# Attention B in another slot order, with the first sequences' rows gathered in the stage before and the last scatters a sequence earlier

## What is computed

```python
x = x + attn_a(layernorm(x))          # 16 heads, 12 of them over a window
x = x + ffn(layernorm(x))             # "first FFN"
x = x + attn_b(layernorm(x))          # "attention B"
x = x + ffn(layernorm(x))             # "second FFN", the same weights

# ffn: 16 experts, four are taken for every row, and a shared one for all rows
hid = relu2(einsum('th,eih->eti', flat, W1)); y = einsum('eti,ehi->eth', hid, W2)
out = einsum('eth,te->th', y, cw) + relu2(flat @ Ws1.T) @ Ws2.T

# attn_b: D = 512, chunks of 128 rows, four of them in a sequence of 512 rows
q, k, v = x @ Wq + bq, x @ Wk + bk, x @ Wv + bv; gate = sigmoid(x @ Wg + bg)
local = softmax(causal(q @ k.T * scale)) @ v       # inside a chunk
cross = q @ (sum of k.T @ v over the earlier chunks)
out = ((local + cross) * gate) @ Wo + bo
```

## Time and profile before

| what | value |
|---|---|
| median of 3 runs | 3603.19 us (3586.75 to 3605.06) |
| profiled execution | 3567.86 us |
| its span | 3566.1 us |
| mean granted TensorE clock | 0.913 |

### The profile page before, as it was taken

The page is one execution under the profiler, slowest core; times in us unless marked ns, Lnnn a source line. Parts: engine busy times, 40 slices in busy tenths (PEclk is TensorE's granted clock), DMA queues, the critical chain, the costliest instruction groups (busy, mean ns, idle before and its releaser), DMA issues. The chain is left out here.

```text
span 3566.1 us, 59187 instructions
## 1 busy us (share of the span) xinstructions
PE 2901.0 (81%) x17728; PEld 2204.3 (62%) x17728; DVE 2236.6 (63%) x5557; ACT 1598.9 (45%) x3092; POOL 1407.1 (39%) x1606
## 2 busy tenths in 40 slices
PE   6989889889977678988749888888888828899982
PEld 4655565555555467878736666666666618778871
DVE  8878777778747567754435656557557344456653
ACT  3554544545542145656524343333433316556650
POOL 2323233233240644443154223555453235545545
PEclk9999999999987689999969999999998959999996
DMA  1211212112013356767632112332332246778873
GB/s 63 79 44 57 71 50 75 48 49 79 37 52 121 130 189 214 241 228 257 215 92 65 54 60 65 101 99 91 99 99 68 68 169 237 256 249 282 287 243 119
DMA packets 206294, 454.65 MB, mean 127 GB/s; under 512 B 28304, under 2 KB 119568, under 8 KB 204944
## 3 DMA queue, kind: packets, MB, share of 16 engines
q1 hardware_dynamic: 156816, 316.37, 26.0%
q0 software_dynamic: 49152, 134.28, 11.5%
HBM read 215.15 MB, written 234.88 MB: 126 GB/s over the span
## 5 line engine op out<-in xcount | busy, mean ns | idle before, releaser
L370 POOL TENSOR_SCALAR_AFFINE_SELECT a_pt<-a_pt 128x512 f32<-128x512 f32 (+1 forms) x320 | 178.3, 557 | 687.9 <-ACT a_pt L470 687.2
L1723 POOL DMA_INDIRECT b_yg<-made,k_picks x256 | 250.7, 979 | 412.6 <-DVE b_xin L1874 342.3
L1024 POOL DMA_INDIRECT slots<-f_xn,k_picks x256 | 254.7, 995 | 329.4 <-PE f_XT L1463 124.8
L470 ACT ACTIVATE a_pt<-a_S 128x384 f32<-128x384 f32 (+3 forms) x640 | 254.7, 452 | 258.7 <-PE a_S L767 255.1
L2461 POOL DMA_INDIRECT f_yg<-made,k_picks x256 | 255.9, 1000 | 233.3 <-PE f_XT L2642 120.3
L617 DVE TENSOR_REDUCE a_mx<-a_FB 128x2 f32<-128x384 f32 (+4 forms) x512 | 276.1, 591 | 51.1 <-PE a_FB L745 37.4
L2187 PE MATMUL b_FB<-b_xh,b_wl 128*128 128x512 f32 x384 | 167.6, 437 | 129.7 <-DVE b_xl L2110 110.4
L1733 POOL DMA_INDIRECT slots<-b_staged,k_picks x192 | 192.5, 1003 | 186.6 <-PE b_FB L2189 71.5
L739 PE MATMUL a_FB<-a_kb,a_qb 128*128 128x192 bf16 (+4 forms) x1024 | 204.2, 264 | 59.7 <-DVE a_mx L617 52.0
L767 PE MATMUL a_S<-a_qs,a_ks 97*128 97x384 f32 (+3 forms) x640 | 180.6, 360 | 35.7 <-ACT a_pt L470 20.4
L780 PE MATMUL a_PV<-a_pt,a_vv 128*32 128x192 f32 (+4 forms) x2048 | 197.1, 367 | 2.7 <-POOL a_pt L377 2.6
(11 more groups left out here) (395 smaller groups left out, 7701.8 us busy)
## 6 DMA issues: line engine op xcount, KB each, us to landing
f_xg<-slots SPq DMA_DIRECT2D x160, 512.0 KB
made<-f_ye SPq DMA_DIRECT2D x160, 512.0 KB
slots<-a_zeros SPq DMA_DIRECT2D x16, 2560.0 KB, 9.2
a_xin<-in_x SPq DMA_DIRECT2D x16, 512.0 KB, 10.1
x_after_a<-a_xres SPq DMA_DIRECT2D x16, 512.0 KB, 2.9
f_xin<-x_after_a SPq DMA_DIRECT2D x16, 512.0 KB
f_wexp<-in_w_exp SPq DMA_DIRECT2D x8, 1024.0 KB, 12.8
bases<-f_xin SPq DMA_DIRECT2D x16, 512.0 KB
```

The lines of the kernel that those rows point to most:

```text
L470: nc.scalar.activation(pt[:, u % 4, b * w:(b + 1) * w], S[:, s_bank[2 * u + b], 0:w], ACT.Exp).then_inc(e_done, 1)
L1024: nc.gpsimd.indirect_dma_start(out=slots[s // BATCH][:, :], out_offset=bass.IndirectOffsetOnAxis(ap=picks[:, i:i + 1], axis=0), in_=xn[:, ...
L1723: nc.gpsimd.indirect_dma_start(out=yg[:, b, k, :], out_offset=None, in_=made[s // BATCH][:, :], in_offset=bass.IndirectOffsetOnAxis(ap=rou ...
```

## The change

The rows of sequences 0 and 1 are gathered on GpSimd in steps 61 to 64 and 68 to 71 of the first FFN; their bases are loaded by SyncE at step 59 into `xin`, and VectorE combines sequence 0 behind steps 63 to 66. `yg` and `xin` are therefore shared by both stages. Attention B starts without them; sequence 1 is combined there in the body of -1. In attention B the front's two T move from slots 2 and 3 to 0 and 1, K and V products alternate, the routing's transposes and logits stand two and one slots later, ranks and choice one. The scatters of sequences 0 to 8 stay where they were; 9 and 10 both go into the body of 14, out of `yg`, which no gather uses any more, and 11 into the body of 15. The last body, 16, has none.

```diff
@@ -846,6 +846,7 @@
...
+        self.yg, self.xin = sb("yg", [P, TB, TOP_K, H]), sb("xin", [P, 2, TB, H])
...
@@ -1009,10 +1013,15 @@
...
+                    if v == G_AT - 2:
+                        for s in range(2):
+                            sp.wait_ge(b_stored[s], 16)
+                            sp.dma_start(xnext[:, s], rows(base_d, s)).then_inc(next_loaded, 16)
...
@@ -1048,6 +1057,18 @@
...
+                def gather(s, b):
+                    if s == 0 and b == 0:
+                        for i in range(2):
+                            pool.wait_ge(ye_stored[i], 16 * NSTEP // 2)
+                    if s:
+                        pool.wait_ge(c_step, TOP_K * (b + 1))
+                    for k in range(TOP_K):
+                        i = s * PICKS + b * TOP_K + k
+                        nc.gpsimd.indirect_dma_start(
+                            out=yg[:, b, k, :], out_offset=None, in_=made[0][:, :],
+                            in_offset=bass.IndirectOffsetOnAxis(ap=picks[:, i:i + 1], axis=0)).then_inc(gathered[b], 16)
...
+                    for s, first in ((0, G_AT), (1, G_AT + TB + 3)):
+                        if first <= T - E_AT < first + TB:
+                            in_step(T)
+                            gather(s, T - E_AT - first)
+                for b in range(TB):
+                    pool.wait_ge(gathered[b], 2 * 16 * TOP_K)
...
@@ -1366,6 +1393,17 @@
...
+                def combine(b):
+                    dve.wait_ge(gathered[b], 16 * TOP_K)
+                    if b == 0:
+                        dve.wait_ge(next_loaded, 32)
+                    for k in range(TOP_K):
+                        j = b * TOP_K + k
+                        if k:
+                            dve.wait_ge(c_step, j)
+                        nc.vector.scalar_tensor_tensor(out=xnext[:, 0, b, :], in0=yg[:, b, k, :], scalar=wall[:, j:j + 1],
+                                                       in1=xnext[:, 0, b, :], op0=ALU.mult, op1=ALU.add).then_inc(c_step, 1)
...
@@ -1401,6 +1439,8 @@
...
+                    if G_AT + 2 <= v < G_AT + 2 + TB:
+                        combine(v - G_AT - 2)
...
@@ -1526,15 +1566,16 @@
...
-    FRONT = [("T", 0), ("T", 1)] + [(c, i) for c in "qkvg" for i in range(DT)]
+    FRONT = ([("T", 0), ("T", 1)] + [("q", i) for i in range(DT)] + [(c, i) for i in range(DT) for c in "kv"] +
+             [("g", i) for i in range(DT)])
...
-    FRONT_SLOT = (2, 3, 4, 5, 6, 7, 8, 9, 10, 11, 12, 13, 14, 15, 16, 17, 18, 19)
...
-    ROUTE_AT = {4: ("rT0", "rT1"), 7: ("rL",), 15: ("rX",)}
+    ROUTE_AT = {6: ("rT0", "rT1"), 8: ("rL",), 16: ("rX",)}
...
@@ -1559,8 +1600,11 @@
...
-    MOMENT_SLOT, RLOG_SLOT, SCALE_SLOT, GROUP_SLOT, CHOOSE_SLOT, PLACE_SLOT, TABLE_SLOT = 15, 1, 2, 10, 11, 16, 17
-    RES_SLOT, SCATTER_SLOT = 8, (9, 12, 15, 18)
+    MOMENT_SLOT, RLOG_SLOT, SCALE_SLOT, GROUP_SLOT, CHOOSE_SLOT, PLACE_SLOT, TABLE_SLOT = 15, 1, 2, 10, 12, 17, 18
+    RES_SLOT, SCATTER_SLOT, SCATTER_SLOTS = 8, (9, 12, 15, 18), (4, 6, 8, 10, 12, 14, 16, 18)
+    LAST = nseq - BATCH - 1
+    SCATTERS = {s: (s - BATCH - 1,) for s in range(BATCH + 1, nseq - 2)}
+    SCATTERS.update({nseq - 2: (LAST - 2, LAST - 1), nseq - 1: (LAST,)})
...
@@ -1682,15 +1727,18 @@
...
-                    if 0 <= s - BATCH - 1 < nseq - BATCH:
-                        at_least(sp, scattered, 16 * PICKS * (s - BATCH - 1))
-                        sp.dma_start(staged[:], seq_rows(sp, xn_d, s - BATCH - 1)).then_inc(st_loaded, 16)
+                    for i in SCATTERS.get(s, ()):
+                        if i in (LAST - 2, LAST - 1):
+                            sp.wait_ge(c_step, PICKS * (nseq - 1))
+                            sp.dma_start(yg[:, LAST - 1 - i], seq_rows(sp, xn_d, i)).then_inc(yg_loaded[LAST - 1 - i], 16)
+                        else:
+                            at_least(sp, scattered, 16 * PICKS * i)
+                            sp.dma_start(staged[:], seq_rows(sp, xn_d, i)).then_inc(st_loaded, 16)
...
-                sp.dma_start(xin[:, 0], seq_rows(sp, base_d, 0)).then_inc(x_loaded, 16)
...
@@ -1707,8 +1755,6 @@
...
-                sp.wait_ge(x_loaded, 16)
-                sp.dma_start(xin[:, 1], seq_rows(sp, base_d, 1)).then_inc(x_loaded, 16)
...
@@ -1716,8 +1762,7 @@
...
-                    if s:
-                        pool.wait_ge(c_step, PICKS * (s - 1) + TOP_K * (b + 1))
+                    pool.wait_ge(c_step, PICKS * (s - 2) + TOP_K * (b + 1))
...
@@ -1727,36 +1772,39 @@
...
-                        pool.wait_ge(st_loaded, 16 * (s + 1))
+                        if s in (LAST - 2, LAST - 1):
+                            pool.wait_ge(yg_loaded[LAST - 1 - s], 16)
+                        else:
+                            pool.wait_ge(st_loaded, 16 * (s + 1 if s < LAST else LAST - 1))
+                    src = yg[:, LAST - 1 - s] if s in (LAST - 2, LAST - 1) else staged
...
-                            in_=staged[:, b, :], in_offset=None).then_inc(scattered, 16)
+                            in_=src[:, b, :], in_offset=None).then_inc(scattered, 16)
...
                 def body(s, par, core, front, ahead):
                     for e in range(NSLOT):
...
-                            pool.wait_ge(c_step, PICKS * (s + 2))
+                            at_least(pool, c_step, PICKS * (s + 1))
...
-                        if e in SCATTER_SLOT and 0 <= s - BATCH - 1 < nseq - BATCH:
+                        mine = SCATTERS.get(s, ())
+                        at = SCATTER_SLOT if len(mine) == 1 else SCATTER_SLOTS
+                        if mine and e in at:
                             if front:
                                 pool.wait_ge(f_done, filled(s + 1, FRONT_AT[e][0]))
-                            scatter(s - BATCH - 1, SCATTER_SLOT.index(e))
+                            scatter(mine[at.index(e) // TB], at.index(e) % TB)
...
-                for s in range(2):
-                    for b in range(TB):
-                        gather(s, b)
...
@@ -1864,13 +1912,13 @@
...
-                    dve.wait_ge(gathered[b], 16 * TOP_K * (s + 1))
+                    at_least(dve, gathered[b], 16 * TOP_K * (s - 1))
                     if b == 0:
-                        dve.wait_ge(x_loaded, 16 * (s + 1))
+                        at_least(dve, x_loaded, 16 * (s - 1))
                     for k in range(TOP_K):
                         j = s * PICKS + b * TOP_K + k
                         if k:
-                            dve.wait_ge(c_step, j)
+                            dve.wait_ge(c_step, j - PICKS)
...
@@ -2149,7 +2197,7 @@
...
-                        if ahead and e in C_SLOT:
+                        if ahead and s + 2 >= 1 and e in C_SLOT:
                             combine(s + 2, C_SLOT.index(e))
```

More of the change, by code:

```diff
@@ L932, in phase_f @@
         ye_stored = [sem("ye_stored%d" % i) for i in range(2)]
+        gathered, next_loaded, c_step = [sem("gathered%d" % i) for i in range(TB)], sem("next_loaded"), sem("c_step")
         NCONST = 12
+        G_AT = NV - NSTEP + 1
         def used(sem, ring, i):
@@ L1651, in phase_b @@
         n_stored, st_loaded, scattered = sem("n_stored"), sem("st_loaded"), sem("scattered")
+        yg_loaded = [sem("yg_loaded%d" % i) for i in range(2)]
         NSTAT = TB + 10
```

11 lines of the change are left out of this document (7 added, 4 removed).

## The result

| what | before | changed |
|---|---|---|
| median (4 runs each, same chip) | 3594.97 us (3582.12 to 3605.06) | 3534.66 us (3526.17 to 3540.37) |
| ratio, 95% interval | | 0.9833, 0.9803 to 0.9863 |
| profiled span, mean granted clock | 3566.1 us, 0.913 | 3538.6 us, 0.919 |

The change is 60 us faster; forecast were 116. The time lies inside the outer range of 3430 to 3555, but outside the 3455 to 3520 that the forecast gave itself. The two profiled executions lie only 27 us apart, because the one of before was a fast one of its kernel (27 us under its median).

The account below looks back on a forecast made before the run. TensorE, busy 81% of the span, was taken to bound the kernel, with time to gain at the handover, in attention B and at its end. Terms -43.5 + 8 - 75 - 5 = -115.5 gave 3487 us, own range 3455 to 3520.

Parts of the forecast that it names:

- Term 1: Handover into attention B: first product 13.8 us behind the first transfer instead of 59.0; minus 43.5 us taken, bounds 35 and 48.
- Term 2: First FFN's last twenty steps: 32 gathers and the combines put in there cost plus 8 us, bounds 0 and 15.
- Term 3: Attention B's sequences: earlier T casts and alternating K and V save 5 us a sequence, fifteen times, 75 us.
- "Fifteen times": Attention B: the 5 us gain of one sequence was counted for all fifteen, giving 75 us.
- The clock: One attention B sequence: a shorter wait before slow-clock products gains 0.7 to 1.3 us, booked as 1.
- "K and V alternate": Attention B: small waits at V and gate products shrink by 1 us; a K copy behind table loads costs 0.7.
- Term 4: End of attention B: scatters moved up a sequence shorten the 10 us with nothing busy; minus 5, bounds 0 and 10.
- A: Rival: attention B's VectorE chain is longer through the shared port lock, 2.4 us in each of fifteen sequences; 3523 us, chance 0.14.
- "it just misses": Attention B: GpSimd's addition ends at 38.4 us of the sequence, VectorE's scaling comes at 38.5, so they do not meet.
- C: Rival: attention B's granted clock stays low for 15 us after each of two waits a sequence; slower, 3703 us, chance 0.04.
- D: Rival: attention B's second T cast still waits for softmax and tables, gain waited at V; 1 us a sequence, 3547, chance 0.08.
- B: Rival: attention B's waits fall below what slows the clock and bank waits go; 3 us more per sequence, 3442, chance 0.12.

Follow-up runs that it names:

- the last experiment: Changed kernel with last scatter group in slot 19, K products ahead of V, and two sequences' scatters moved from body 14 to 15: 3463.93 us, 0.9739 of the kernel before.
- the best kernel: Changed kernel with the last scatter group in slot 19 instead of 18 and K products ahead of V again: 3453.81 us, 0.9719 of the kernel before.
- the order alone: Kernel before with only attention B's new slot order; gathers, combine, handover and scatters as before: 3524.60 us, 0.9895 of the kernel before.

## Why the prediction was right in direction and twice too large

**Term 1, handover (-43.5): right, measured -39.0.** The first product stands 15.5 us behind the first transfer, 13.8 were forecast, released by the second weight piece's low half, as said; the wait for piece 3 is 1.45 us (1.7). D(0) comes 28.3 us behind the first product instead of 23.8, with a wait of 1.1 at a copy of V and a clock of 0.90.

```profile
1805.88 2.35 POOL L1810 TENSOR_TENSOR b_wl<-b_raw,b_wh 128x1024 fp32r<-128x1024 f32 x1 [3.67 <-ACT b_wh L1858]
1808.33 0.77 PE L2235 MATMUL b_FB<-b_xh,b_wl 128*128 128x512 f32 x1 [3.24 <-POOL b_wl L1810]
...
1819.46 0.47 PE L2235 MATMUL b_FB<-b_wh,b_xl 128*128 128x512 f32 x1 [1.45 <-POOL b_wl L1810]
```

**Term 2, the first FFN (+8): right in kind, about 12.** Four executions without the gathers took 155 to 166 us from the thirtieth-last load, ten with them 167 to 181: means 161.2 and 172.9. At the first gathers a tile load comes late; whether the gathers or the two row loads issued just ahead of them (1688.5), which the prediction had at nothing, hold it up, no run separates. Behind that each of the four steps with a combine takes 4.7 to 5.0 us instead of 4.4, since the tile's copy on VectorE stands behind it. Both in the changed kernel:

```profile
1698.12 1.09 PE L1503 MATMUL f_XT<-k_ident,f_xg 128*128 128x128 f32 x8 [2.04 <-DMA f_xg<-slots]
...
1711.87 2.04 DVE L1405 SCALAR_TENSOR_TENSOR k_xin<-k_yg,k_wall,k_xin 128x256 f32<-128x256 f32 x4
...
1715.85 0.66 PE L1503 MATMUL f_XT<-k_ident,f_xg 128*128 128x128 f32 x4 [0.38 <-DVE f_xe L1383]
```

**Term 3, fifteen sequences (-75): this failed, measured -18.4 and -15.8.** Its working of one sequence was good where no scatters stand: first product at 12.1 (12.2 forecast, though its parts add up to 12.0), 1.89 us of wait (2), V's fourth product 1.9 to 2.6 (3). Only K was off, 1.6 to 2.3 instead of 0.7. Three steps failed:

- "Fifteen times". The sequences with scatters were given the five of the others. There GpSimd's run of eight holds the release of softmax and first T, to +5.3 to +5.5 in five of the six sequences. The prediction looked at scatters only as GpSimd's time ("free"), and read sequence 8 in the old spacing, where the softmax was released at +3.9. The three sequences behind a table gained 1.7 each on average, sequence 0 nothing.
- The clock. It was booked as a gain of about one. Where the wait for the low half stayed at 2.7 us and that for K at 2.3 to 2.5, products ran at 0.63 us behind them, the lower level: 14 to 18 of them in sequences 7, 8, 11 and 12. What such spells cost shows in the last experiment: its sequences 1 and 2 have 6.5 and 6.3 us of waits, 21 and no products of 128x512 at 0.6 us or more, a granted clock of 0.92 and 1.00, and take 63.1 and 58.1 us.
- "K and V alternate" (+1 - 0.7). It leaves a wait of 1.6 to 2.3 us for K and one of up to 2.6 at V's fourth product even where the signals are on time. Without it, in the best kernel, three of mostly 1.1 to 1.3 stand there, and its ten sequences with neither table nor double scatters have no slow product.

With spacing and alternation put right the fifteen sequences gained 72, about the forecast's 75, though by another road: 5.8 to 8.1 in each of the ten sequences with neither table nor double scatters, 66.6 in all, and 6.5 in the three behind a table together.

**Term 4, the end (-5): right in kind, about -11.** 85 to 91 us in four executions without it, 75 to 79 in seven with it. The second FFN's first transfer follows VectorE's last operation at once (2876.66, 2876.94), so all of the 10 us went; I had kept five for a stage's change.

**Sum.** -39 + 12 - 18 - 11 = -56, beside 60 and 55 measured. The second FFN, unchanged by the diff, took 637 to 662 us from one execution to another, with means that differ by 3, and the part ahead of the gathers 1598 to 1617; this covers the differences of single profiles, and I read nothing into it. Terms 1 and 3 are from single traces, 2 and 4 from means of several, so that the sum comes near is a support and no proof.

**The rivals.** A, the lock: its operation, VectorE's scaling of the mean, took 275 ns at most in sixteen, where it had been 3035. But other short operations of the same chain met GpSimd's addition: in 5 and 7 to 12 of the changed kernel one of them took 2.7 to 2.9 us instead of 0.16. In sequence 8:

```profile
2381.66 2.79 DVE L2122 TENSOR_TENSOR b_mean<-b_stats 128x4 f32<-128x4 f32 x1
2382.01 2.41 POOL L1794 TENSOR_TENSOR b_xres<-k_xin,b_bo 128x1024 f32<-128x1024 f32 x1
```

The rule quoted (Trainium skill, "SBUF — State Buffer", section "SBUF: two separate sides") has one of the two wait for the whole of the other, and the trace agrees: VectorE's operation ends with the addition. The recorded starts do not say who holds the ports, since VectorE's is the earlier one here. The prediction read its row too narrowly: in the kernel before, three operations of the chain met the addition in turn, one in each of sequences 1 to 12, where the prediction had fewer than half. And "it just misses" held only in 1 to 4 and 6, where the addition starts at +37.2 to +38.4; in 5 and 7 to 12 it starts at +39.7 to +46.7.

The late addition belongs to a chain that I followed through nine traces of the new slots (the two that spread or leave out gathers are not among them; sequences 1 to 4, 6 to 8 and 10 to 12, ninety in all). Behind a wait of 2.6 to 2.7 us for the low half the first products ran at the lower level in 18 of 20 sequences, behind one of 2.3 to 2.5 in 3 of 10, behind one of 1.9 in 12 of 60. Where they did, the last gathers and the addition came later, and in 30 of these 33 the addition started behind +41. All 30 met the lock and took 63.1 to 67.4 us; the 57 with no slow product there had the addition at +37.1 to +38.6 and took 58.0 to 62.8. Three of these 57 met the lock all the same, at +36.5 to +36.6, and took 58.2 to 59.4. So what the late release brings is above all the longer wait ahead of the first product, and with it this chain. No run moved the addition alone, so the lock's own share in these longer sequences is open, and why the same wait of 1.9 us was followed by slow products in one sequence and not in the next is open too; A's time, 3523, being near is no sign for its 2.4 us in each sequence. C, the granted clock, came true in part, in single sequences, not as 15 us in each. D named a loss at V and a sum near the measured one, 3547, but its cause is absent: the wait for the second T's low half shrank from 5.4 to 5.7 us to 1.9 to 2.7. B, more than the forecast, did not come.

## What to carry over

A transfer queue that has room is not free: look at how an engine's indirect transfers are grouped, and whether the waiters of other engines are released on time beside them. In a timeline, take the producer's end from the waiter's start; a wait put down to "remote", or two engines released within 0.1 us of each other by different products, is the sign. Their count alone says little of the time: the order alone had 42 such waits, the changed kernel 46. Look at a whole group of short operations for a lock, not at one of them. And rather than shift a wait, split it: behind three of 1.2 us the clock stayed, behind one of 2.6 it often fell, and the slow spells, not the idle time, made the 5 us between two such sequences.
